# Two steps of a square layer made together instead of one after the other

## What is computed

```python
xn = layernorm(x)
x + attention(xn) + ffn(xn)          # attention: 16 heads, linear (elu + 1), its own layernorm and residual

def ffn(xn):                         # weights are -1, 0 or 1; s are scales by output column
    h = silu(tlin(xn, w1_w, w1_s)) * tlin(xn, w2_w, w2_s)     # 256 -> 1024
    h = gelu(tlin(h, h1_w, h1_s))                             # 1024 -> 1024
    h = gelu(tlin(h, h2_w, h2_s))                             # 1024 -> 1024
    return tlin(h, w3_w, w3_s)                                # 1024 -> 256
```

## Time and profile before

| | us |
|---|---|
| median of 3 runs | 1477.41 (1475.27 to 1477.58) |
| the profiled execution | 1476.11 |
| its span | 1474.3 |
| of it PE busy | 1465.8 |
| DVE, ACT, POOL busy | 1161.3, 935.6, 466.8 |
| one tile of the loop | 90.70 |

### The profile page before, as it was taken

The page is one execution under the profiler, slowest core; times in us unless marked ns, Lnnn a source line. Parts: engine busy times, 40 slices in busy tenths (PEclk is TensorE's granted clock), DMA queues, the critical chain, the costliest instruction groups (busy, mean ns, idle before and its releaser), DMA issues.

```text
span 1474.3 us, 33305 instructions
## 1 busy us (share of the span) xinstructions
PE 1465.8 (99%) x11020; PEld 1269.2 (86%) x11020; DVE 1161.3 (79%) x2090; ACT 935.6 (63%) x1727; POOL 466.8 (32%) x554
## 2 busy tenths in 40 slices
PE   9999999999999999999999999999999999999998
PEld 5997988979798797988979889798897988979887
DVE  6857778787887877878788787887878878787787
ACT  4556657666575766757657666575765667666564
POOL 2213415234151341504325043240523415234141
PEclk9999999999999999999999999999999999999999
DMA  8796845727366373663727548185481854827444
GB/s 239 233 311 238 281 145 182 259 93 269 127 215 231 105 266 114 237 212 113 259 110 264 185 141 286 58 278 174 147 297 47 279 170 165 277 68 253 160 160 158
DMA packets 85058, 287.66 MB, mean 195 GB/s; under 512 B 7456, under 2 KB 45984, under 8 KB 61728
## 3 DMA queue, kind: packets, MB, share of 16 engines
q0 software_dynamic: 43296, 231.75, 46.0%
q1 hardware_dynamic: 40896, 54.29, 11.2%
q10 hardware_dynamic: 832, 1.18, 0.2%
HBM read 270.42 MB, written 25.17 MB: 200 GB/s over the span
## 4 chain that ended last, share of the span: by engine, by line
PE 99%; DVE 1%; ACT 0%; issue 0%; DVEq 0%; ACTq 0%
PE ps L1042 53%; PE ps L1015 8%; PE ps L1013 7%; PE ps L1127 7%; PE ps L902 4%; PE ps L904 4%; PE ps L903 4%; PE ps L1075 4%; PE ps L965 2%; PE ps L954 2%; PE ps L975 1%; PE ps L924 1%; PE ps L1098 1%; PE ps L896 0%; PE ps L1152 0%; DVE values_a L1736 0%
## 5 line engine op out<-in xcount | busy, mean ns | idle before, releaser
L1042 PE MATMUL ps<-operands_a,hidden_weights 128*128 128x256 f32 x2520 | 367.9, 285 | 0.0
L1042 PE MATMUL ps<-lo_a_in_bits,hidden_weights 128*128 128x256 f16 x2520 | 337.1, 273 | 0.0
L1042 PEld LDWEIGHTS ps<-operands_a,hidden_weights 128*128 128x128 f32 x2520 | 323.5, 189 | 1.4 <-DVE partial_sums L1783 0.2
L1783 DVE TENSOR_TENSOR partial_sums<-partial_sums,ps 128x512 f32<-128x512 f32 x300 | 204.2, 685 | 119.4 <-PE ps L1042 69.2
L1745 DVE SCALAR_TENSOR_TENSOR lo_a_in_bits<-values_a,operands_a 128x512 f16<-128x512 f32 x315 | 236.6, 773 | 42.0 <-POOL values_a L775 20.5
L1042 PEld LDWEIGHTS ps<-lo_a_in_bits,hidden_weights 128*128 128x128 bf16 x2520 | 232.6, 98 | 35.1 <-DVE lo_a_in_bits L1745 3.2
L783 POOL DMA_DIRECT2D hidden_weights<-weight_blocks x236 | 135.6, 575 | 383.4 <-PE ps L1042 359.4
L1383 ACT ACTIVATE operands_a<-values_a 128x512 fp32r<-128x512 f32 x180 | 112.9, 627 | 70.3 <-POOL values_a L760 18.9
L760 POOL TENSOR_TENSOR values_a<-values_a 128x512 f32<-128x512 f32 x30 | 38.4, 1281 | 357.1 <-DVE values_a L1736 338.1
L1015 PE MATMUL ps<-xnT,w_ffn 128*128 128x512 f32 x512 | 150.5, 421 | 0.0
L1042 PE MATMUL ps<-operands_b,hidden_weights 128*128 128x256 f32 x840 | 146.8, 296 | 0.0
(11 more groups left out here) (162 smaller groups left out, 2735.6 us busy)
## 6 DMA issues: line engine op xcount, KB each, us to landing
hidden_weights<-weight_blocks POOLq DMA_DIRECT2D x180, 1024.0 KB, 5.3
hidden_weights<-weight_blocks POOLq DMA_DIRECT2D x60, 512.0 KB, 3.9
raw_weights<-weight_blocks SPq DMA_DIRECT2D x42, 347.5 KB, 3.0
hidden_weights<-in_w_ffn POOLq DMA_DIRECT2D x16, 512.0 KB, 8.0
weight_blocks<-weight_sums SPq DMA_DIRECT2D x16, 512.0 KB, 3.3
weight_blocks<-in_w_ffn SPq DMA_DIRECT2D x16, 512.0 KB, 10.3
out_dram<-acc SPq DMA_DIRECT2D x31, 256.0 KB, 2.2
x<-in_H SPq DMA_DIRECT2D x15, 512.0 KB, 5.4
```

The source lines that it names most:

```text
L1042: r = mm(bank[:, m * HT:(m + 1) * HT], wk, xk, start=i in firsts and begins and m == 0 and j == 0, stop=i in lasts and ends and m == 1 and ...
L1783: v.tensor_tensor(scratch[:, dst, :], scratch[:, kept, :], product_bank(s, i), ALU.add).then_inc(add.sem, 1)
```

## The change

Steps 0 and 1 are made together, and steps 2 and 3. `products(t, pair, i, parts)` takes the place of `product`: for product i it makes the eight high matmuls of the even step, the eight of the odd step, then the eight low ones of each. The order is P1, P5, P6, P7, P2, P3, P4 for both pairs, always high first. The interleaving by hand at the start of step 0 is gone; `to_rows` stands after P5, `proj_step` after P6 of the first pair, the next tile's `transposes` after P6 of the second.

The weights' blocks stand in DRAM in the order in which the products need them (`PAIRED`: step 0's P1, step 1's P1, step 0's P5, and so on), so a turn of the ring is no longer a step: turn 0 ends with step 0's P7, turn 1 begins with step 1's P7. The odd step keeps its partial sums in the gate ring and in one new buffer (`second_partial_sum`). POOL makes all eight differences of H0 and H1. `check_piece` has six smaller pieces. DVE, ACT and POOL get new orders; `ln2_normalise`, `ln2_gain_and_shift` and `ln2_sum` move forward.

```diff
-RING_ORDER = (1, 5, 6, 7, 2, 4, 3)
+ORDER = (1, 5, 6, 7, 2, 3, 4)
+PAIRED = tuple((s, i) for p in range(2) for i in ORDER for s in (2 * p, 2 * p + 1))
 RING_PARTS = ((0, 1), (1, 2), (3, 2), (5, 2))
...
+    def ring_place(s, i):
+        return PAIRED.index((s, i)) % PRODUCTS
+
+    def ring_turn(s, i):
+        return PAIRED.index((s, i)) // PRODUCTS
...
+    def ring_part_free(t, turn, g):
+
+        s, i = PAIRED[turn * PRODUCTS + sum(RING_PARTS[g]) - 1]
+        return prod.after(t, f"{s}P{i}")
...
-                def product(t, s, i, parts=HI_FIRST):
-
-                    quarter_product(t, s, i, 0, parts[0], begins=True)
-                    quarter_product(t, s, i, 1, parts[0])
-                    quarter_product(t, s, i, 0, parts[1])
-                    quarter_product(t, s, i, 1, parts[1], ends=True).then_inc(prod.sem, 1)
+                def products(t, pair, i, parts):
+
+                    for part in parts:
+                        for s in (2 * pair, 2 * pair + 1):
+                            quarter_product(t, s, i, 0, part, begins=part == parts[0])
+                            r = quarter_product(t, s, i, 1, part, ends=part == parts[1])
+                            if part == parts[1]:
+                                r.then_inc(prod.sem, 1)
```

More of the change, by code:

```diff
@@ L413, in block_kernel @@
     h_made = Count(sem("gated_value_made"), HC, HC)
-    add = Named(sem("products_added"), tuple(f"{s}{c}" for s in range(4) for c in ADDS[s]))
+    add = Named(sem("products_added"), ADDS)
     lo_half = Named(sem("lo_made"), LO)
-    dve_t = Named(sem("difference_made_by_dve"), DVE_T)
     pool_t = Named(sem("difference_made_by_pool"), POOL_T)
@@ L764, in t2 @@
                 pool.wait_ge(*difference_made(t, group, "T1"))
+                if group == "H1":
+                    pool.wait_ge(*prod.after(t, "1P4"))
                 tt(value(group, "T2"), value(group, "B22"), value(group, "T1"), ALU.subtract).then_inc(pool_t.sem, 1)
@@ L1585, in body @@
[L1585 to L1597 removed]
+                    transposed_hi(t + 1, 1)
@@ L1797, in add_w @@
-            def add_w(t, s, more=True):
-                second_sum(t, s, 7, more)
-            def add_v(t, s):
-                second_sum(t, s, 5)
+            def add_w(t, s):
+                if s >= 2:
+                    dve.wait_ge(*gelu.after(t, f"{s - 2}C22"))
+                sum_into(t, s, 7, 2, 0)
             def add_c22(t, s):
-                dve.wait_ge(*add.after(t, f"{s}w" if s % 2 == 0 else f"{s}v"))
-                sum_into(t, s, 5 if s % 2 == 0 else 7, 2, 2)
+                dve.wait_ge(*add.after(t, f"{s}w"))
+                sum_into(t, s, 5, 2, 2)
@@ L2101, in body @@
                     lo(t, "G1", "B21", first > 0)
+                    rows_lo(t, 0)
+                    rows_lo(t, 1)
+                    add_u(t, 0)
+                    add_u(t, 1)
+                    lo(t, "G0", "B22", first > 0)
+                    lo(t, "G1", "B22", first > 0)
+                    if more:
+                        ln1_stats(t + 1)
                     add_w(t, 0)
+                    add_w(t, 1)
+                    add_c22(t, 0)
+                    add_c22(t, 1)
                     lo(t, "G0", "T4", first > 0)
@@ L2104, in body @@
                     lo(t, "G1", "T4", first > 0)
-                    add_c22(t, 0)
-                    lo(t, "G0", "B22", first > 0)
-                    lo(t, "G1", "B22", first > 0)
-                    rows_lo(t, 0)
-                    add_c12(t, 0)
-                    add_c21(t, 0)
+                    ln2_stats(t)
                     if checking and more:
                         check_piece(t - 1, 0)
-                    rows_lo(t, 1)
-                    if more:
-                        ln1_stats(t + 1)
@@ L2117, in body @@
-                    add_u(t, 1)
-                    ln2_stats(t)
-                    add_v(t, 1)
+                    add_c12(t, 0)
+                    add_c12(t, 1)
                     lo(t, "H0", "B11", first > 0)
+                    lo(t, "H1", "B11", first > 0)
+                    add_c21(t, 0)
+                    add_c21(t, 1)
                     lo(t, "H0", "T1", first > 0)
+                    lo(t, "H1", "T1", first > 0)
                     lo(t, "H0", "T2", first > 0)
-                    add_c22(t, 1)
@@ L2147, in body @@
-                    add_c12(t, 2)
-                    if not more:
-                        ln2_gain_and_shift(t)
+                    add_u(t, 2)
                     add_u(t, 3)
-                    if checking and not more:
-                        check_rest()
-                    if not more:
-                        ln2_sum(t)
+                    lo(t, "H0", "T4", first > 0)
+                    lo(t, "H1", "T4", first > 0)
+                    lo(t, "H0", "B21", first > 0)
+                    lo(t, "H1", "B21", first > 0)
```

368 lines of the change are left out of this document (150 added, 218 removed).

## The result

The changed kernel takes 1576.99 us (median of 4 runs, 1572.73 to 1582.53) against 1477.03 for the kernel before in the same comparison: the ratio is 1.068, with a 95% interval of 1.064 to 1.072. I had forecast 1492. The direction was right; the size was not: +100 us instead of +14, about 6.5 us a tile instead of 1.0. The profiled execution took 1572.73, its span is 1570.9.

What follows compares the result with a forecast made beforehand. PE, 99% busy, bounds the kernel. A tile: -0.33 + 1.3 + 0.05 = +1.0; fourteen +14, last tile +0.2, so the profiled 1476.11 becomes 1490.3 and the median 1491.6, say 1492; range 1482 to 1506.

Steps and rivals of the forecast that it cites:

- What the longer runs give: PE's square layers: products made as fourteen pairs gain 0.33 us a tile, with 0.2 and 0.5 as ends.
- The ring wait: Step 3's P1: PE waits for its weight load, issued behind ln2's inverse root on POOL, 1.3 us a tile (0.9 to 1.7).
- `rows_lo`: At `proj_step`: DVE's `rows_lo` has no slack, costing PE 0.05 us a tile, or 0.5 if ACT is late.
- T1 and T2 of H1 move to POOL: Second layer: POOL has them ready at about 32, PE wants them with P5 at 33.4; cost nothing.
- `ln2_gain_and_shift` and `ln2_sum` move forward: End of the tile, ahead of the last sums on DVE: cost taken as 0, with 0.5 us as the other end.
- Further waits add up: Rival: `proj_step`, part 2's load and ACT's end of the tile cost 0.9 us a tile more, 1505 us; chance 0.18.

Runs made afterwards that it cites:

- experiment 10: Experiment 4's kernel, fourth check back where the change put it, ACT's rows_hi ahead of residual and G1's T4: 1501.96 us; ahead of G1's T4 only: 1474.39 us.
- experiment 7: Experiment 4's kernel with POOL's inverse root of ln2 put back ahead of the loads of parts 1 and 2: 1534.53 us.
- experiment 1: The changed kernel with POOL's inverse root of ln2 moved behind the loads of parts 1 and 2 of turn 2: 1588.18 us.
- experiment 3: The changed kernel with ln2's inverse root behind the two loads, and ln2's sums and the fourth check moved back to the end: 1543.93 us.
- experiment 4: Experiment 3's kernel with all eight differences of H0 and H1 moved from POOL to DVE: 1486.06 us.
- experiment 8: The changed kernel with one edit alone, the eight differences of H0 and H1 made by DVE: 1577.41 us.
- experiment 5: Experiment 4's kernel with six more differences on POOL between its loads, which nobody reads: 1566.50 us.

## Why the prediction was wrong, step by step

- **What the longer runs give** was right within its ends. I took 0.33 a tile, 0.2 to 0.5; it is 0.44 where nothing waits (experiment 10). Pairs of runs are 3.66, as forecast from the earlier trace rows.
- **The ring wait** was right in place and mechanism and a little too small: 25.7 us in 15 waits, 1.7 each, against 1.3 (0.9 to 1.7). In the tile that I read, counted from 721.29: `ln2_stats` ends at 25.7 (I had 25.3; 0.45 of it is the wait of `proj_step`), the inverse root takes 1.43 and 0.2 and ends at 27.5 (I took 1.43 for both together, from the earlier trace rows), the load is issued 0.50 later, not 0.3, and lands 4.9 later, as in the earlier trace rows. What I left out is what a wait of this length does to the clock: alone, in experiment 7, the term costs 48 us and not 28.
- **`rows_lo`**: I took 0.05, with 0.5 as the end. It is 0.45 in each of 14 tiles. In the tile that I read `rows_lo` ends at 12.4 (I had 12.1), and `proj_step` starts 0.25 behind it, a release that I had added at the ring but not here. The end, not the value, should have gone into the sum.
- **T1 and T2 of H1 move to POOL: "Free."** This is the step that failed. I costed only when the results are ready, and named as the cover the length of P1. With the load's wait ahead of it that cover did hold in the changed kernel: PE waits for no low part there, and it is the sums of u, behind the held low parts on DVE, that it waits 20.3 us for. What POOL's running does to DVE I did not cost at all, though the trace before showed it three times a tile: a low part of 1.70 and two of 1.1 beside a difference, against 0.69 for the others. The change stands all eight differences in rows, and those hold a low part for 3.1 to 4.1 us in the changed kernel and up to 6.0 in experiments 1 and 3. Without the other two causes this costs 58 us (experiments 3 and 4). I even argued the other way, that DVE "has POOL idle beside it": true up to `ln2_stats`, and false right behind it.
- **`ln2_gain_and_shift` and `ln2_sum` move forward: 0, at most 0.5.** Also failed. I took half a us, "a piece of DVE's work or two", as the upper end, but three instructions of 1.2 us each stand there, ahead of sums for which ACT stands idle 4.19 us; moved back, they give 42 us. I had written that DVE is nearly full there, and did not draw the conclusion that whatever is put ahead costs most of its length (42 us are 3.0 a tile, of 3.8).
- **The rivals.** "Further waits add up", at 0.18, came nearest, and was priced far too low (1505): it took 0.9 us a tile for three small slacks, not for a DVE that is 5 us late. Its argument against itself, that the first wait gives later ones their time back, is true in one sense: the three causes hide one another (experiments 1 and 8), which is why 6.5 us a tile and not their sum was lost. That the time rose, as forecast, owes something to luck: of the 80 us of waits only the load's 25.7 come from the chain that I had worked out.

How much of the 100 us belongs to each cause can't be said as a sum, since undoing one alone gives -11, 0 and +42. What is shown is what each costs where the others are gone: the load's term 48 (experiments 4 and 7), POOL's differences, all eight of H0 and H1, 58 (experiments 3 and 4). For ln2's sums that was not run on the best kernel; moved back in the changed kernel they give 41.9, and together with the check's place 44.2 (experiments 1 and 3) and 42.9 (experiments 8 and 7).

## What to carry to other kernels

When work moves to another engine, cost not only when its result is ready but also what the engine's running does to its neighbour: look in the trace for instructions that are longer beside it than elsewhere, and count how many of its instructions will stand in a row. A wait that is removed is worth nothing while a second late place stands behind it, so undo the suspects together once before judging them one by one. On an engine that is nearly full, an instruction put ahead of one that is waited for can cost most of its length: here 3.0 of 3.8 us.

## What was not expected of the hardware

- A DVE instruction with two inputs in SBUF that begins beside POOL's differences ends 0.50 to 0.57 us after the end of one of them. Mostly that is the last of a row, and not the first: 4.05, 5.93 and 6.23 us instead of 0.68. A gap of 0.54 in POOL's row, in which it issued a load, did not let it in (836.20 to 836.74 in experiment 3). But in the changed kernel 34 low parts and checks were held for two or three differences, and 9 low parts got in after the first of two that stand back to back, as that at 757.72 did. What decides it stays open.
- It works in the other direction too: POOL's differences beside such DVE instructions are up to 1.8 us long instead of 1.28 (3.52 for two in experiment 5).
- A wait of PE of about 2 us was followed by a stretch at 1.2 GHz in eight tiles of fourteen (experiment 7), each 1.7 us longer; the waits of 0.45 a tile in experiment 4 were not (granted clock 0.999 over the whole run).
